# Expert down rows in rounded products where no shared unit follows, four more shared units among the experts, and other banks and a later finishing for the late blocks

## What is computed

```python
gx = xp[buf_tok]                                   # 64 x 128 rows of 512
gu = jnp.einsum('ech,ehi->eci', gx, gate_up_proj)  # 64 experts, 512 x 384
g, u = jnp.split(gu, 2, axis=-1)
hid = jax.nn.silu(g) * u
eo = jnp.einsum('eci,eih->ech', hid, down_proj) * buf_w[..., None]   # 192 x 512
routed = jnp.zeros((T + 1, h), x.dtype).at[buf_tok.reshape(-1)].add(eo.reshape(-1, h))[:T]
shared = jax.nn.silu(xf @ shared_gate_w.T) * (xf @ shared_up_w.T) @ shared_down_w.T
return (routed + shared).reshape(b, s, h)
```

## Time and profile before

| | |
|---|---|
| median of 3 runs | 916.13 us (914.24 to 916.36) |
| the profiled execution's own time | 912.62 us |
| its span | 910.9 us |
| busy in it: TensorE matmuls, weight loads | 891.4 us, 726.2 us |
| VectorE, ScalarE, GpSimd | 719.0, 548.3, 486.2 us |

### The profile page before, as it was taken

How to read it: one execution, slowest core, us unless ns; L and a number is a source line. 1 busy time by engine, 2 the same in 40 slices (tenths; PEclk the granted TensorE clock), 3 DMA queues, 4 the chain that set the end, 5 groups by cost and what they waited for, 6 DMA issues and landing times. The chain is left out here.

```text
span 910.9 us, 15578 instructions
## 1 busy us (share of the span) xinstructions
PE 891.4 (98%) x4626; PEld 726.2 (80%) x4626; DVE 719.0 (79%) x1421; ACT 548.3 (60%) x1208; POOL 486.2 (53%) x540
## 2 busy tenths in 40 slices
PE   9999999999999999999999999999999999999996
PEld 7788887888888788777888788888888888877875
DVE  6997887979788897898867788787878887736676
ACT  5532544435353443535548878888878788736784
POOL 2002366566566656677434566665566666433664
PEclk9999999999999999999999999999999999999999
DMA  6344553536263343539567999999999999959973
GB/s 203 105 162 116 130 153 102 129 91 178 74 189 96 119 107 104 156 88 343 182 229 228 330 364 345 366 337 318 350 356 360 353 343 315 287 116 391 379 245 116
DMA packets 116242, 203.95 MB, mean 224 GB/s; under 512 B 18496, under 2 KB 56384, under 8 KB 115136
## 3 DMA queue, kind: packets, MB, share of 16 engines
q1 hardware_dynamic: 95632, 159.87, 51.2%
q0 software_dynamic: 19520, 35.75, 16.2%
q10 hardware_dynamic: 1008, 7.34, 2.0%
HBM read 143.03 MB, written 59.88 MB: 223 GB/s over the span
## 5 line engine op out<-in xcount | busy, mean ns | idle before, releaser
L1587 POOL DMA_INDIRECT slot_table<-tokens,slot_of x162 | 180.2, 1113 | 86.9 <-issue 50.5
L1632 POOL DMA_INDIRECT acc_rows<-eo,table_sb x64 | 135.5, 2117 | 118.5 <-DMA acc_rows<-eo,table_sb 64.0
L1687 PE MATMUL bank<-x_hi,wqkv_hi 128*128 128x512 f32 x384 | 152.1, 396 | 0.3 <-DVE wqkv_lo L1010 0.3
L1687 PE MATMUL bank<-x_lo,wqkv_hi 128*128 128x512 f32 x384 | 150.2, 391 | 0.0
L1687 PE MATMUL bank<-x_hi,wqkv_lo 128*128 128x512 f32 x384 | 150.1, 391 | 0.0
L1442 DVE TENSOR_TENSOR wgu_lo<-wgu,wgu_hi 128x1536 fp32r<-128x1536 f32 x64 | 112.0, 1752 | 2.5 <-ACT wgu_hi L905 1.9
L905 ACT CAST wgu_hi<-wgu 128x1536 fp32r<-128x1536 f32 x64 | 94.2, 1474 | 1.6 <-issue 0.4
L1621 POOL DMA_INDIRECT xg<-x_rows,table_sb x64 | 74.3, 1161 | 36.2 <-issue 18.7
L1687 PE MATMUL bank<-wgu_hi,xgt_hi 128*128 128x384 f32 x256 | 91.3, 357 | 0.0
L675 ACT ACTIVATE e<-bank 128x512 f32<-128x512 f32 x64 | 38.0, 593 | 79.6 <-PE bank L1687 79.6
L1687 PE MATMUL bank<-wgu_lo,xgt_hi 128*128 128x384 f32 x256 | 85.7, 335 | 0.0
(11 more groups left out here) (195 smaller groups left out, 2295.0 us busy)
## 6 DMA issues: line engine op xcount, KB each, us to landing
wgu<-w_gu SPq DMA_DIRECT2D x64, 768.0 KB, 7.6
wdn<-w_down SPq DMA_DIRECT2D x64, 384.0 KB, 8.4
xres<-x SPq DMA_DIRECT2D x32, 256.0 KB, 3.3
x_turned<-x1t SPq DMA_DIRECT2D x32, 256.0 KB
x_rows<-x SPq DMA_DIRECT2D x32, 256.0 KB, 3.4
acc_rows<-x SPq DMA_DIRECT2D x32, 256.0 KB, 3.4
fin<-acc_rows SPq DMA_DIRECT2D x8, 1024.0 KB, 11.8
odd<-acc_rows SPq DMA_DIRECT2D x8, 1024.0 KB, 13.9
```

Of the source, the lines that this page charges most:

```text
L1587: pool.indirect_dma_start(table_dram, bass.IndirectOffsetOnAxis(slot_of[:, i, k:k + 1], 0), tokens[:, i:i + 1], None, bounds_check=SLOTS - ...
L1632: pool.indirect_dma_start(acc_dram[e % 2], bass.IndirectOffsetOnAxis(table_sb[:, e:e + 1], 0), eo[eo_slot[e]][:, :], None, bounds_check=T ...
L1687: mm = pe.matmul(out_ap, a, b, start=first and i == 0, stop=final and i == len(products) - 1)
```

## The change

Four things. The plain down rows are split like all others in each expert behind which no shared unit stands (`split_first`). `HEAD` goes from 2 to 6, so that 24 units stand among the experts (one each) and 26 in the tail; the experts without a unit are 40, before 44. The down rows of late blocks get banks of their own, four that the experts used (`tail_ps`); so those of block 4 wait until all experts' rows are scaled (`eo_done`), and those of later blocks for the finishing of the same tile of the block before. And in the tail a pair is finished three units later than it is made (`PAIR_BEHIND`), but for the last block's, `EARLY_AFTER` is a new table, and the split of the next block's `x1t` goes ahead of the pair.

```diff
+    wdn_hi = [late.place(f"wdn_hi{i}", [P, D], F32R) for i in range(2)]
+    het_hi = [late.place(f"het_hi{i}", [P, 2 * P], F32R) for i in range(2)]
+    het_lo = [late.place(f"het_lo{i}", [P, 2 * P], F32R) for i in range(2)]
+    wdn_lo = [Map(nc, at, at + 4 * D).place(f"wdn_lo{i}", [P, D], F32R) for i, at in enumerate(wdn_at)]
...
-    HEAD = 2
+    HEAD = 2 * SC
...
+    def split_first(e):
+        return not fills_of[e]
+
...
-    EARLY_AFTER = {**{i: 1 for i in range(8, 14)}, **{i: 1 for i in range(16, 22)}, **{i: 1 for i in range(24, 28)}}
+    EARLY_AFTER = {**{i: 1 for i in range(12, 17)}, **{i: 1 for i in range(19, 25)}, 27: 2, 28: 2, 29: 1}
...
+    PAIR_BEHIND = 3
+
+    def pairs_after(i):
+        u = i if i >= UNITS_LEFT - NJ // 2 else i - PAIR_BEHIND
+        done_at_once = u != i and u >= UNITS_LEFT - NJ // 2
+        return 1 if u >= HEAD and u % UNITS >= 2 * SC and not done_at_once else 0
...
+        tail_ps = [banks[3], banks[4], banks[5], banks[7]]
...
+        def shared_ps(b, j):
+            return proj_ps[rows_take[b, j] % 3] if b < EARLY else tail_ps[j]
...
+                if split_first(e):
+                    act.copy(wdn_hi[e % 2][:, :], w[:, 0:D])
...
-                act.copy(hid_et[e % 2][:, :], ht_ps[:, 0:P])
-                act.copy(het_hi[e % 2][:, :], ht_ps[:, P:2 * P]).then_inc(het_hi_done, 1)
+                if split_first(e):
+                    act.copy(het_hi[e % 2][:, :], ht_ps[:, 0:2 * P]).then_inc(het_hi_done, 1)
+                else:
+                    act.copy(hid_et[e % 2][:, :], ht_ps[:, 0:P])
+                    act.copy(het_hi[e % 2][:, P:2 * P], ht_ps[:, P:2 * P]).then_inc(het_hi_done, 1)
...
+                if split_first(e):
+                    dve.tensor_tensor(wdn_lo[e % ND][:, :], w[:, 0:D], wdn_hi[e % 2][:, :].bitcast(F32), ALU.subtract)
...
+                cols = slice(0 if split_first(e) else P, 2 * P)
+                dve.tensor_tensor(het_lo[e % 2][:, cols], ht_ps[:, cols], het_hi[e % 2][:, cols].bitcast(F32),
                                   ALU.subtract).then_inc(het_lo_done, 1)
...
-                if i % UNITS >= 2 * SC:
+                if i % UNITS == 2 * SC and EARLY + i // UNITS + 1 < NB:
+                    split_x1t(EARLY + i // UNITS + 1)
+                for _ in range(pairs_after(i)):
                     finish_pair(added)
                     added += 2
-                if i % UNITS == 2 * SC and EARLY + i // UNITS + 1 < NB:
-                    split_x1t(EARLY + i // UNITS + 1)
...
-                        if not late_chunk:
-                            pe.wait_ge(*freed[take - 3])
+                        if not late_chunk and b < EARLY:
+                            pe.wait_ge(*freed[rows_take[b, j] - 3])
+                        elif not late_chunk and b > EARLY:
+                            pe.wait_ge(fin_added, fin_no[b - 1, j] + 1)
+                        elif not late_chunk:
+                            pe.wait_ge(eo_done, NE)
...
-                chain(eo_ps[:, :], [(hid_et[e % 2][:, :], wdn_buf[e % ND][:, 0:D])], first=False).then_inc(eo_mm, 1)
+                if split_first(e):
+                    products = three(het_hi[e % 2][:, 0:P], het_lo[e % 2][:, 0:P], wdn_hi[e % 2][:, :], wdn_lo[e % ND][:, :])
+                else:
+                    products = [(hid_et[e % 2][:, :], wdn_buf[e % ND][:, 0:D])]
+                chain(eo_ps[:, :], products, first=False).then_inc(eo_mm, 1)
```

More of the change, by code:

```diff
@@ L92, in build @@
     wgu_buf = [both.place(f"wgu{i}", [P, KC, GU]) for i in range(2)]
+    wdn_at = [both.at + 4 * i * DN for i in range(2)]
     wdn_buf = [both.place(f"wdn{i}", [P, DN]) for i in range(2)]
@@ L201, in build @@
     wgu_buf += [late.place(f"wgu{i}", [P, KC, GU]) for i in range(2, NG - 1)]
+    wdn_at += [late.at + 4 * i * DN for i in range(ND - 3)]
     wdn_buf += [late.place(f"wdn{i}", [P, DN]) for i in range(2, ND - 1)]
@@ L216, in build @@
     hid_et = [late.place(f"hid_et{i}", [P, P]) for i in range(2)]
-    het_hi = [late.place(f"het_hi{i}", [P, P], F32R) for i in range(2)]
-    het_lo = [late.place(f"het_lo{i}", [P, P], F32R) for i in range(2)]
     assert late.at <= kept_from
@@ L297, in build @@
     assert done == total
+    def split_first(e):
+        return not fills_of[e]
     early = [(b, j) for b in range(EARLY) for j in range(NJ)]
     UNITS_LEFT = TAIL * UNITS
-    EARLY_AFTER = {**{i: 1 for i in range(8, 14)}, **{i: 1 for i in range(16, 22)}, **{i: 1 for i in range(24, 28)}}
+    EARLY_AFTER = {**{i: 1 for i in range(12, 17)}, **{i: 1 for i in range(19, 25)}, 27: 2, 28: 2, 29: 1}
     assert sum(EARLY_AFTER.values()) == len(early)
-    fin_order = []
-    for i in range(HEAD, UNITS_LEFT):
-        if i % UNITS >= 2 * SC:
-            pair = i % UNITS - 2 * SC
-            fin_order += [(EARLY + i // UNITS, j) for j in (2 * pair, 2 * pair + 1)]
-        fin_order += [early.pop(0) for _ in range(EARLY_AFTER.get(i, 0))]
+    PAIR_BEHIND = 3
[3 more added lines that the diff above has]
+        return 1 if u >= HEAD and u % UNITS >= 2 * SC and not done_at_once else 0
+    fin_order = []
+    for u in range(HEAD, UNITS_LEFT):
+        for _ in range(pairs_after(u)):
+            m = u if u >= UNITS_LEFT - NJ // 2 else u - PAIR_BEHIND
+            pair = m % UNITS - 2 * SC
+            fin_order += [(EARLY + m // UNITS, j) for j in (2 * pair, 2 * pair + 1)]
+        fin_order += [early.pop(0) for _ in range(EARLY_AFTER.get(u, 0))]
     fin_no = {tile: n for n, tile in enumerate(fin_order)}
@@ L1254, in finish_pair @@
                     dve.wait_ge(down_mm, NJ * b + j + 1)
[L1255 removed]
+                    add_shared(n + t, shared_ps(b, j)[:, :], joined[t])
                     if n + 2 == NFIN:
@@ L1836, in unit @@
                             products += three(hid_hi[:, c, tok], hid_lo[:, c, tok], sd_hi[:, c, :], sd_lo[:, c, :])
-                        mm = chain(proj_ps[take % 3][:, :], products, first=not late_chunk, final=late_chunk)
+                        mm = chain(shared_ps(b, j)[:, :], products, first=not late_chunk, final=late_chunk)
                         if late_chunk:
@@ L1920, in down @@
                     pe.wait_ge(eo_done, e)
-                products = [(part[e % 2][:, :], wdn_mix[e % 2][:, :]) for part in (het_hi, het_lo)]
+                products = [(part[e % 2][:, P:2 * P], wdn_mix[e % 2][:, :]) for part in (het_hi, het_lo)]
                 chain(eo_ps[:, :], products, final=False)
-                chain(eo_ps[:, :], [(hid_et[e % 2][:, :], wdn_buf[e % ND][:, 0:D])], first=False).then_inc(eo_mm, 1)
+                if split_first(e):
[3 more added lines that the diff above has]
+                chain(eo_ps[:, :], products, first=False).then_inc(eo_mm, 1)
             for _ in range(BEFORE_EXPERTS[0]):
```

11 lines of the change are left out of this document (4 added, 7 removed).

## The result

The changed kernel took 923.75 us in the median (921.47 to 928.63, 4 runs), the kernel before, beside it on the same chip, 915.18 us (912.78 to 916.36, 4 runs). The ratio is 1.0113, with a 95% interval from 1.0088 to 1.0138: slower. The profiled execution took 921.47 us with a span of 919.7, against 912.6 and 910.9.

A forecast was written before the change was run, and what follows sets the result against it. TensorE was taken to bound both stages, with VectorE and ScalarE close behind. Experts +10.0 us and tail -4.6 us gave +5.4: 918.0 us profiled, 921.5 us median, range 914 to 927.

The forecast's parts named there:

- split, less TensorE work: Expert stage: three rounded products replace the plain one in 40 experts without a unit, saving 0.16 us each, 6.4 us.
- waits that the split adds: Expert stage: later xgt_lo adds 3.7 us at second experts without a unit and 3 us at next such experts' first products.
- gathers and second N experts that the units relax: Expert stage: 10.9 us more stage with the same loads removes 1.2 of 6.5 us of TensorE's gather waits.
- waits for the finishing and `hid_lo` gone: Tail: with four banks, TensorE's waits for finishing (1.8 us) and for hid_lo (1.2 us) go, -3.0 us.
- unit 22: Tail: VectorE has 15.1 to 18.0 us of work against TensorE's 13.7; wait of +2.0 us, from 0 to 4.
- unit 30: Tail: VectorE's queue before unit 29's hid_lo, 16.6 to 19.5 us against 13.7, makes TensorE wait 5.4 us (2.9 to 5.8).
- behind the last matmul: Kernel's end: the last rows leave VectorE with its queue full, +0.9 us.
- the step on the second N: Second of two experts without a unit (N): transposes 0.16 us earlier, xgt_lo 0.13 later; wait from 0.16 to 0.43 us.
- VectorE's sum of work: Each expert without a unit: VectorE's work rises from 3.83 to 4.56 us, against TensorE's 3.9 to 4.1.
- TensorE as the only bound: Rival, whole kernel: VectorE's new work fits its 43 us of waiting; -6.4 us, some 910 us; 10% chance.
- The transfers: Rival: loads set the expert stage, so moved units cost only +1 to +5 us; 912 to 917 us; 12% chance.
- VectorE and ScalarE bound at their bounds: Rival: both bound every expert without a unit, and tail waits reach 5.8 and 4 us; +12, 928 us; 15% chance.

The follow-up runs named there:

- kernel 2: The changed kernel without the split, down rows plain in all experts; ratio 1.0085 to the kernel before.
- kernel 1: The kernel before with only the split, in all 44 experts without a shared unit; ratio 1.0006 to the kernel before.
- kernel 8: The split alone on the kernel before, without VectorE's subtraction for wdn_lo (TensorE reads wdn_hi instead, result lacks the low part); ratio 0.9988 to the kernel before.
- kernel 9: The kernel before with plain down products replaced by three rounded matmuls on tiles already there, no copy or subtraction, another result; ratio 0.9965 to the kernel before.
- kernel 12: kernel 10 with VectorE's wgu_lo ahead of het_lo in experts without a shared unit; 907.88 us, ratio 0.9933 to the kernel before.
- kernel 4: The changed kernel with pairs finished one unit behind in place of three; 925.75 us, ratio 1.0055 to the kernel before.
- kernel 5: The changed kernel with pairs one unit behind and early tiles spread, one behind each of units 11 to 21 and 24 to 28; ratio 1.0039 to the kernel before.
- kernel 7: The changed kernel with unread matmuls filling TensorE's waits, 8 at unit 22 and 26 at unit 30; ratio 1.0081 to the kernel before.
- kernel 11: kernel 6 with most late pairs finished at once or one unit behind, and the early tile behind unit 13 moved to unit 29; ratio 1.001 to the kernel before.
- kernel 6: kernel 5 with HEAD 5, three units moved among the experts in place of four; ratio 0.9993 to the kernel before.
- kernel 3: The kernel before with only the late blocks' four banks and their waits; ratio 0.9995 to the kernel before.
- kernel 10: The kernel before (HEAD 2, no split) with four banks, the change's x1t order, and the first late block's pairs one unit later; ratio 0.9977 to the kernel before.

## Why the prediction was right, and where its steps were not

The time (921.5 against 923.75) and the sign were right, and a part of that is luck: errors in the two stages went against each other. The experts were put 2.6 us too high, the tail with what lies behind it 6.6 us too low.

| term | forecast, us | measured |
|---|---|---|
| split, less TensorE work | -6.4 | -6.4 (0.856 to 0.69 per expert) |
| waits that the split adds | +6.7 | +6.2 (6.4 less the 0.2 of kernel 2) |
| gathers and second N experts that the units relax | -1.2 | -3.3 (7.6 of 10.9) |
| waits for the finishing and `hid_lo` gone | -3.0 | -3.0 |
| `eo` at the tail's start | +1.0 | +0.99 |
| unit 22 | +2.0 | +3.6 |
| unit 30 | +5.4 | +7.7 |
| matmuls at the lower clock | none | +3.4 |
| behind the last matmul | +0.9 | +0.1 |

**The stage of the experts.** The three products, `wdn_lo` (686 ns), `het_lo` (425), `wdn_hi` (622) came as read from their nearest rows. That the split pays nothing was right in sum, as kernels 1 and 2 show, and so was the step on the second N: transposes that come 0.16 us earlier and an `xgt_lo` that comes later. Before, I read one of these waits, 0.16 us, and counted 20; the trace has 16 of 0.10 to 0.31 us, 3.6 in all, beside three that a gather ends. The step that failed is the other one, VectorE's sum of work: 4.56 us against TensorE's 3.9, which I used against the fast rival and for 3 us of waits at the next N's first product. No such wait came. The split adds 3.2 us in front of the transposes and 3.3 us at the down rows of nine experts, where `het_lo` is late. Kernel 8 takes 0.60 us of the work away and the pair stays; kernel 9 takes all of it away and TensorE still waits. The order on VectorE behind ScalarE's `het_hi` set the pair, and kernel 12 shows it from the other side. I had written that I am wrong if the wait before `het_lo` soaks up the new work in the second N too. It did for `wdn_lo`, as kernel 8 shows, and the loss stayed: work ahead of that wait is soaked up, but what stands behind it in the queue can't use it. The clue stood in the earlier trace rows: idle 0.90 us, then 1.75 us of `wgu_lo`, then the `xgt_lo` that TensorE waits for.

**The relaxed gathers** gave more than I took: the waits of the earlier trace rows went but for one of 1.1 us.

**The tail.** This is the larger miss, 2.0 us longer in place of 4.6 shorter. The mechanism at unit 30 was right and its size low. I put 16.6 to 19.5 us of VectorE's work into 13.7 us. The row shows a `hid_lo` that waits 3.01 us for ScalarE behind the same tiles, where the longest such wait of the tail was 1.8 us before. I had named ScalarE's share and taken less than its bound. Kernels 4 and 5 show whose wait it is: it stays when pairs move, and falls from 6.3 to 1.7 us when the early tiles spread. Unit 22 was underestimated in the same way. And I had no term for the clock: 15 matmuls at 0.43 us and a few in between, 3.4 us. Of these the 1.9 at unit 30 only hid GpSimd's lateness. Without them 9.8 us lie behind the last matmul (kernel 7), 2.0 more than before, where I had +0.9.

**The rivals.** TensorE as the only bound would have needed no chain on VectorE: kernel 9, the nearest to it, gives back 3.2 us. The transfers did not set the stage: it grew by 7.6 us for 10.9 us of work, and the waits for gathers are most of the difference. The case of VectorE and ScalarE bound at their bounds came nearest at unit 30.

## What to carry to other kernels

Where an engine idles ahead of one operation and is late with the next but one, read its queue between the two: an operation of no urgency that stands behind the wait costs its full length there, and ahead of the wait it can be nearly free (here 0.1 us in half of the places). A kernel that gets the gain without its price (here the split without its subtraction and copy) tells a chain from an overloaded engine before the real edit is written. Work that is pushed towards the end of a queue is to be costed on every engine that takes part in it, and what a long wait then does to TensorE's clock goes on top where TensorE still sets the time behind it (1.5 us at unit 22, nothing at unit 30).

## What the runs showed of the hardware

I had not expected the clock. TensorE was busy 97% of the changed kernel's span. After some of its idle times the granted clock was 0.50, the level of 1.2 GHz, and a 128x512 matmul took 0.427 us from start to start where it took 0.227. After others it stayed at 1.00. The granted clock in a window right behind such a wait:

| TensorE idle before it, us | granted clock behind it |
|---|---|
| 6.93 (change, unit 30), 6.98 (kernel 2), 3.42 (kernel 11, a gather) | 0.50 |
| 2.77 (kernel 6, unit 22), 2.75 (change, unit 22) | 0.52, 0.56 |
| 2.78 (kernel 2, unit 22), 2.75 (kernel 11, unit 22) | 1.00 |
| 2.27 (kernel 9), 2.22 (kernel 3), gathers | 0.50 |
| 2.17 (kernels 8 and 10), gathers | 1.00 |
| 1.50 (kernel 6), 1.61 (kernels 10 and 12) | 1.00 |
| 1.49, and 0.82 some 2 us later (kernels 4 and 5) | 0.50 |
| the same two (change, kernel 7) | 1.00 |

```profile
878.30:881.70 3.40, 3.38 (x15) 2.78 (x16) 3.31 (x7) 3.40 (x7) 1.79 (x3) 1.00 0.85 325
881.20:884.50 3.30, 3.30 (x15) 2.73 (x16) 3.21 (x7) 3.30 (x7) 1.75 (x3) 1.00 1.05 406
655.40:658.70 3.30, 3.30 (x13) 3.30 (x11) 2.46 (x3) 1.61 (x5) 1.05 (x1) 0.50 1.05 402
```

The lines are kernel 2, kernel 11 and kernel 9. The same wait of 2.75 us in the same place was followed by either level, so the length of one idle time does not decide it in these runs, and what does stays open. The Trainium skill (TensorE: Matmul & The Clock Gate, Wait — 56ns, not 53.3ns?) has 426.7 ns for a back-to-back matmul of 512 columns at 1.2 GHz, and the trace agrees. It has 215.7 ns at 2.4 GHz, where the rows here have 227; the sums go by the rows.

A wait filled with 26 matmuls of no use kept the clock at 1.00 (kernel 7). At unit 30 this bought no time, since GpSimd was late too.
